# Two-layer relational graph convolution on one core: four places for the one-hot tile S, and the five spreads of counts laid out over seven quads of a half-lap

## What is computed

```python
edge_type = argmax(msg[:, 16:26])                       # 10 types
sums = segment_sum(x[src], dst * 10 + edge_type)        # per node and type
mean = sums / maximum(count, 1)
layer(x) = einsum('nrd,rdo->no', mean, w_rel) + x @ root + bias
h = relu(layer1(x)); y = layer2(h)
out = layernorm(x + y)                                  # over 128 channels
```

## Time and profile before

| | |
|---|---|
| median of 3 runs | 4677.97 us (4676.41 to 4679.4) |
| the profiled execution, its own time | 4682.32 us |
| its span, first to last instruction | 4680.6 us |
| POOL busy | 2997.3 us (64%) |
| PE busy | 2485.8 us (53%) |
| DVE busy | 1887.6 us (40%) |
| ACT busy | 365.6 us (8%) |
| mean granted TensorE clock | 0.712 |

### The profile page before, as it was taken

How to read it: one execution, slowest core, us unless ns; L and a number is a source line. 1 busy time by engine, 2 the same in 40 slices (tenths; PEclk the granted TensorE clock), 3 DMA queues, 4 the chain that set the end, 5 groups by cost and what they waited for, 6 DMA issues and landing times.

```text
span 4680.6 us, 32772 instructions
## 1 busy us (share of the span) xinstructions
PE 2485.8 (53%) x10947; PEld 1812.4 (39%) x10948; DVE 1887.6 (40%) x2168; ACT 365.6 (8%) x397; POOL 2997.3 (64%) x3139
## 2 busy tenths in 40 slices
PE   3556566565656656565644454544445454444446
PEld 2334444343434444444433233333333333333334
DVE  4444444444445444443523333333333333333334
ACT  1001000010100001010000000000101000000100
POOL 7666666666666666666466666666666666666662
PEclk6667677776767667676776776777777676766777
DMA  4222222222222222222121222111222212121221
GB/s 117 63 64 77 71 65 80 63 83 64 72 76 66 80 65 83 64 66 70 54 56 50 55 54 55 54 54 53 57 54 56 54 53 56 53 56 52 57 55 34
DMA packets 151574, 293.70 MB, mean 63 GB/s; under 512 B 61619, under 2 KB 82503, under 8 KB 147958
## 3 DMA queue, kind: packets, MB, share of 16 engines
q0 software_dynamic: 100032, 205.07, 16.7%
q1 hardware_dynamic: 46630, 87.29, 5.7%
q10 hardware_dynamic: 4867, 0.79, 0.1%
HBM read 264.68 MB, written 28.25 MB: 63 GB/s over the span
## 4 chain that ended last, share of the span: by engine, by line
another core or an unknown queue 47%; DVE 23%; PE 16%; issue 11%; DVEq 3%; ACT 0%; DMA 0%; SPq 0%; ACTq 0%
PE ps_agg L1805 7%; DVE S L2160 7%; DVE ring L2173 6%; PE ps_out L1881 5%; DVE mean L2217 3%; DVE z_end L2198 2%; DVEq L2291 2%; PE ps_bc L1823 2%; PE ps_agg L1800 1%; PE ps_out L1876 1%; DVEq L2173 1%; DVE hit L2154 0%; DVEq L2169 0%; DVE stat L2233 0%
## 5 line engine op out<-in xcount | busy, mean ns | idle before, releaser
L1394 POOL DMA_INDIRECT rows<-table,idx_s x1563 | 1485.8, 951 | 831.7 <-issue 458.7
L1394 POOL DMA_INDIRECT rows<-in_x_dram,idx_s x1507 | 1449.9, 962 | 767.7 <-issue 445.0
L1805 PE MATMUL ps_agg<-S,rows 128*128 128x130 f32 (+3 forms) x6256 | 1531.4, 385 | 251.2 <-issue 250.3
L1805 PEld LDWEIGHTS ps_agg<-S,rows 128*128 128x128 f32 x6256 | 1240.4, 239 | 464.8 <-issue 381.2
L2173 DVE TENSOR_TENSOR ring<-ps_agg,ring 128x429 f32 (+1 forms) x782 | 456.4, 584 | 1849.8 <-remote 1483.7
L2160 DVE TENSOR_TENSOR S<-ps_iota,comb_b 128x1600 f32<-128x1600 f32 x392 | 712.5, 1818 | 96.8 <-issue 95.0
L1823 PE MATMUL ps_bc<-rc_b,sel 74*128 74x448 bf16 x540 | 202.9, 469 | 938.6 <-DVE mean L2217 561.2
L1800 PE MATMUL ps_agg<-zero_b 128*128 128x429 bf16 (+1 forms) x782 | 322.8, 413 | 626.5 <-DVE S L2160 343.3
L2217 DVE TENSOR_TENSOR mean<-ps_bc,ring 128x896 f32<-128x896 f32 (+2 forms) x284 | 300.9, 1061 | 746.3 <-remote 689.9
L1881 PE MATMUL ps_out<-mean,wall 128*128 128x448 f32 (+1 forms) x1120 | 558.3, 627 | 69.0 <-DVE mean L2217 37.5
L1823 PEld LDWEIGHTS ps_bc<-rc_b,sel 74*128 74x128 bf16 x540 | 44.7, 112 | 1000.7 <-DVE mean L2217 589.1
(11 more groups left out here) (158 smaller groups left out, 686.5 us busy)
## 6 DMA issues: line engine op xcount, KB each, us to landing
attr<-in_edge_attr_dram SPq DMA_DIRECT2D x27, 1176.0 KB
rows<-table,idx_s POOLq DMA_INDIRECT x1563
rows<-in_x_dram,idx_s POOLq DMA_INDIRECT x1507
x_in<-in_x_dram SPq DMA_DIRECT2D x54, 224.0 KB
table<-h_s SPq DMA_DIRECT2D x54, 224.0 KB
table<-outT SPq DMA_DIRECT2D x27, 224.0 KB
xt_s<-table SPq DMA_DIRECT2D x27, 224.0 KB
out_dram<-h_s SPq DMA_DIRECT2D x27, 224.0 KB
```

The source lines that it names most:

```text
L1394: pool.indirect_dma_start(out=rows[:, o, j, :], out_offset=None, in_=(x, table)[l][:, :], in_offset=bass.IndirectOffsetOnAxis(ap=at, axis= ...
L1805: ins = t_.matmul(sums[:, :, lo:lo + w], lhsT=rows[:, o, jj, :], rhs=S[:, (par + o) % 2, jj, :].rearrange("p (r n) -> p r n", n=WN)[:, :, ...
```

## The change

- S has four places, `PLACE = (0, 1, 2, 3, 0, 1, 2)` by oct. DVE makes S two octs ahead: in step o for oct o + 2, for o from 0 to 4; in step 6 for octs 0 and 1 of the next half-lap, both ahead of oct 6's sums. To find the room, some rows used only at the start are laid into `mean` and `S`.
- Before each quad PE now waits for `added` of the quad that used its bank two octs ago, since S no longer guards the bank.
- The spreads stand behind quads (1,0), (2,0), (2,1), (3,1), (4,0) and the transform's parts behind (2,1), (3,0), (3,1), (4,1), (5,0); `turn_back` behind (5,1) and no longer (4,1). DVE's scales move with them: k = 0 and 1 in steps 1 and 2 ahead of the sums, 2 and 3 in steps 2 and 3 behind them, 4 in step 4 ahead. The last half-lap of a layer keeps its old tables.
- In layer 2 `centre` moves from step 5 to step 6, `spread_of` to step 0 of the next half-lap, `normalise` to step 1.

The number of instructions on PE, DVE, ACT and POOL stays the same but for one more S made at the start.

```diff
+PLACE = (0, 1, 2, 3, 0, 1, 2)
...
-        S = sb("S", [P, 2, GT, TCOL])
+        S = sb("S", [P, 4, GT, TCOL])
...
-                SPREADS = {(1, 0): 0, (1, 1): 1, (2, 0): 2, (2, 1): 3, (3, 0): 4}
-                TYPES = {(2, 0): (-1, 0, 1), (2, 1): (2, 3), (3, 0): (4, 5), (3, 1): (6, 7), (4, 0): (8, 9)}
+                SPREADS = {(1, 0): 0, (2, 0): 1, (2, 1): 2, (3, 1): 3, (4, 0): 4}
+                TYPES = {(2, 1): (-1, 0, 1), (3, 0): (2, 3), (3, 1): (4, 5), (4, 1): (6, 7), (5, 0): (8, 9)}
...
                             for h in range(quads_of(b, o)):
+                                if o > 1:
+                                    pe.wait_ge(added[o - 2][h], with_it)
+                                elif l or some:
+                                    pe.wait_ge(added[o + 5][h], before)
                                 aggregate(l, b, par, o, h)
...
-                                if some and (o, h) == ((3, 1) if last else (4, 1)):
+                                if some and (o, h) == ((3, 1) if last else (5, 1)):
                                     turn_back(0, HN, past)
...
+                MEANS = {1: 0, 2: 1, 4: 4}, {2: 2, 3: 3}
...
-                            if o < OCTS - 1:
-                                used = (agg_ready[o - 1], with_it) if o else (agg_ready[OCTS - 1], before)
-                                make_S(par, o + 1, None if l == 0 and is_(b, 0) and o == 0 else used, sl)
-                            elif not last:
+                            if o < OCTS - 2:
+                                first = l == 0 and is_(b, 0) and o < 2
+                                make_S(par, o + 2, None if first else (agg_ready[o - 2], with_it) if o > 1 else
+                                       (agg_ready[(6, 3)[o]], before))
+                            elif o == OCTS - 1 and not last:
...
-                                make_S(1 - par, 0, (agg_ready[o - 1], with_it), sl)
+                                for k in range(2):
+                                    make_S(1 - par, k, (agg_ready[4 + k], with_it))
...
-                                elif o == 5 and not last:
+                                elif o == 6 and not last:
                                     centre(b - 1, HN, nth, None if is_(b, 1) else (nth - 1 if known else dve.snap(nth - 1)),
```

More of the change, by code:

```diff
@@ L1272, in gnn_kernel @@
         rows = sb("rows", [P, OCTS, GT, C])
-        S = sb("S", [P, 2, GT, TCOL])
+        S = sb("S", [P, 4, GT, TCOL])
+        first_q = S[0:1, 3, :, :].rearrange("a j c -> a (j c)")[:, 0:QUADS]
         comb_b = sb("comb_b", [P, 2, HT])
@@ L1283, in gnn_kernel @@
         rc_m = sb("rc_m", [R, HN], BF16)
-        rising = mean[:, :, :].rearrange("p r n -> p (r n)")[:, 0:CHUNKS * P].rearrange("p (k c) -> p k c", c=P)
+        mean_f = mean[:, :, :].rearrange("p r n -> p (r n)")
+        rising = mean_f[:, 0:CHUNKS * P].rearrange("p (k c) -> p k c", c=P)
+        row_u = mean_f[0:1, CHUNKS * P:CHUNKS * P + 3 * QUADS]
+        half_row, lap_row, low_row, high_row = (
+            mean_f[0:1, CHUNKS * P + k * QUADS:CHUNKS * P + (k + 1) * QUADS] for k in range(3, 7))
         wall = [sb(f"wall{l}", [P, R, C]) for l in range(2)]
@@ L1952, in _ @@
                             for h in range(quads_of(b, o)):
+                                if o > 1:
+                                    pe.wait_ge(added[o - 2][h], with_it)
+                                elif l or some:
+                                    pe.wait_ge(added[o + 5][h], before)
                                 aggregate(l, b, par, o, h)
-                                if some and (o, h) in SPREADS:
-                                    spread(l, SPREADS[o, h], past, times)
+                                spreads = END_SPREADS if last else SPREADS
+                                if some and (o, h) in spreads:
+                                    spread(l, spreads[o, h], past, times)
                                 types = END_TYPES if last else TYPES
                                 if some and (o, h) in types:
-                                    if o == 2 and h == 0:
+                                    if -1 in types[o, h]:
                                         if l == 0:
@@ L2279, in _ @@
                 dve.wait_ge(comb_ready, 1)
-                make_S(0, 0, None, 0)
+                make_S(0, 0, None)
+                make_S(0, 1, None)
                 for l in range(2):
@@ L2318, in _ @@
                                 hold(b)
-                                make_S(1 - par, 0, (agg_ready[o - 1], with_it), sl)
-                            if some and o in (1, 2, 3):
-                                scale(b, 1 - par, 0, HN, 2 * o - 2, None if l == 0 and is_(b, 1) else prev, past)
+                                for k in range(2):
+                                    make_S(1 - par, k, (agg_ready[4 + k], with_it))
+                            ahead_of, behind = END_MEANS if last else MEANS
+                            if some and o in ahead_of:
+                                scale(b, 1 - par, 0, HN, ahead_of[o], None if l == 0 and is_(b, 1) else prev, past)
                             if o == 5 and not (l == 0 and is_(b, 0)) and not (l == 1 and last):
@@ L2341, in _ @@
                                             None if is_(b, 1) else (prev * 16 if known else dve.snap(prev * 16)))
-                            if some and o in (1, 2):
-                                scale(b, 1 - par, 0, HN, 2 * o - 1, None, past)
+                            if some and o in behind:
+                                scale(b, 1 - par, 0, HN, behind[o], None, past)
                             if some and o == 1 and par == 0:
@@ L2374, in _ @@
                         dve.wait_ge(comb_in, 1)
-                        make_S(0, 0, (agg_ready[OCTS - 2], HALVES), 0)
+                        for k in range(2):
+                            make_S(0, k, (agg_ready[4 + k], HALVES))
                     else:
```

19 lines of the change are left out of this document (8 added, 11 removed).

## The result

The changed kernel takes 4665.18 us (median of 10 runs, 4658.6 to 4668.0), the kernel before beside it 4678.92 us (10 runs, 4670.57 to 4688.76). The ratio is 0.9964 with a 95% interval of 0.9956 to 0.9973: 0.36% faster, 14 us where the forecast had 182. The profiled execution took 4668.0 us, its span 4666.3.

The account below looks back on a forecast made before the run. POOL's gather stream and its stops (642 us of 4682) were taken as the bound; one of three 3.8 us stops gone in 48 of 55 half-laps saves 182 us, giving 4500 us, range 4320 to 4710 us.

Parts of the forecast that it names:

- What bounds the kernel: Both layers' loops: POOL's gather stream sets the pace, and stops in it make up the rest, 642 us.
- The floor of 4040 us: Execution time were POOL never to stop, 4682 - 642 us, since the change removes no gather.
- S two octs ahead: PE's waits for S, 3.6 and 8.9 us a half-lap in layers 1 and 2: half taken off.
- Spreads apart: PE's waits for scales: work moved ahead of spreads fills about 4 us; octs 2 and 3 reached 4 to 8 us sooner.
- The sum: POOL's three stops a half-lap become two in most: 48 of 55 half-laps gain 3.8 us, 182 us together.
- The sign that I had named for being wrong: As many POOL stops with fewer waits for S, meaning the gather stream itself makes the signals late.
- The rival "nothing changes": Late signals come only when gathers cease, so POOL stops as often as before; 4660 to 4690 us, chance 0.14.
- The slower rival: Half-lap's tail: scale 4, `clear`, `take_out`, `turn_back` end later, delaying signals by up to 4.9 us; 4775 to 4870 us, chance 0.15.

Follow-up runs that it names:

- the last chip: Chip number 7: the kernel before and the changed kernel timed again, neither altered; 3984.69 us and 3977.02 us, ratio 0.9981.
- The two halves measured alone: Against the kernel before: four places of S made two octs ahead, old order otherwise, ratio 0.9985; the new order with two places of S, ratio 0.9991.

## Why the prediction was wrong

- **What bounds the kernel** was right: POOL's stream and the stops in it, 642 us; and on the last chip the stops alone are gone, 4679 us against 3985. The floor of 4040 us was near the time without stops.
- **"S two octs ahead" and "Spreads apart"** came as said in layer 2, where the waits for S fell to a quarter and those for scales by half; half of it turned into waits for `added`, which I had put at nothing. In layer 1 the waits for scales grew. One size was misread: a pair of types takes the whole 3.19 us of its row, not 1.6, so what is moved ahead of the fourth spread is some 5.5 us and not 4. That would have made the gain larger, so it is not what failed.
- **The sum** is the step that failed: "three stops a half-lap become two in most", 182 us. They stayed at 160 waits of 3.8 us. I had the mechanism of it in the rows (a late signal comes only when the gathers cease) and still let PE's progress decide how many stops there are. Half of PE's sums gone saves 73 us, four of five round trips some 14 us, the change 14 us: PE's order is worth what these are, not a stop a half-lap. The sign that I had named for being wrong is the one that came: as many stops with fewer waits for S (152.8 us, before 343.3).
- **The rival "nothing changes"**, 0.14, has the mechanism that held; the time 4665.18 us lies in its 4660 to 4690. What I held against it, that PE had run out of work in the stops, was true and no argument: it had run out because its signals were held.
- **The slower rival** did not come: the wait for `turn_back`'s input fell to 42.8 us.
- **Where the 14 us are from**: by the groups by line, the idle time before the gathers of the two layers is 6.5 us less (1592.9 after 1599.4) and the gathers' own time 7.9 us less (2927.8 after 2935.7), in one trace of each kernel. The two halves measured alone, 0.15 and 0.09%, and the 0.19% on the chip without stops fit a small gain of PE's order; what it is wasn't traced.

What the runs support about the stops: the first late signal of a series belongs to work that ends when POOL has issued without a break for 11 to 13 us (median of 67 series in the changed kernel's layer 1; 10 to 13 in the others with 42 or 56 gathers and no breaks put in, 16 with half of PE's sums), and it passes after POOL has stopped. Three stops a half-lap, with some 11 to 13 us of prompt signals behind each and 3.8 us in each, make 44 to 50 us, near the 48.9 us that PE and DVE need when the stream is half. That would explain why bytes, rows, room and order change nothing, why 42 gathers need the same stops as 56, and why breaks every 10 us replace them. It fits; it is not shown. Why a signal of PE's is held on the other chips and not on number 7 stays open, and with it whether the recording of signals has a part in it.

## What to carry to other kernels

When an engine's releaser reads "remote" and the restart follows a stop of another engine, ask first whether the signals are late rather than the work: halve the suspected stream in one run, before any order is changed. One such run (2773 us against 4645) would have told more than all the waits that I added up. Count also how many of the signals that a program raises its trace holds: 23% with the stops and nearly all without them was there to be seen. And time a close change on more than one chip: what is 14% of a time on one can be absent on the next.

## What was not expected of the hardware

- The kernel before took 4640 to 4685 us on three chips and 3985 us on a fourth. The changed kernel's traces have gathers of the same length on both kinds; the difference is stops behind late signals of PE (0 of 919 late, 55% of 784 elsewhere).
- On those three chips PE's signals are late, by 16 us in the place shown, when gathers are issued without a break, while DVE's arrive (none of 634 late). With half of the gathers and other work of POOL's between them none is (0 of 826).
- The traces with late signals hold 19 to 39% of the signals of the gathers, the one from the fourth chip 49971 of 50016. Whether the recording causes the stops was not tested.
- A gather instruction costs POOL 1.25 us with 128 rows of 512 bytes and with 128 of 256, and 1.24 us with 64 rows (0.905 + 0.33 us): fewer or smaller rows buy nothing.
- Twice the room for the gathers, with rows of half the length, made the kernel 18% slower (5460 us against 4645).
